# Cross attention with split fp32: three score banks and one bank of values, values scaled by one multiplication a pair, and the value burst last in TensorE's step

## The reference

```python
N, C, S, H = 16, 64, 256, 8          # after reshape; queries from x, keys and values from ctx
xn  = (x - mean(x[n])) * rsqrt(var(x[n]) + 1e-5) * gamma + beta
q   = Wq @ xn + bq                   # 8 heads of 64 channels
k,v = Wkv @ ctx + bkv
att = softmax((q * C**-0.25) . (k * C**-0.25))     # per sequence n and head, 256 x 256
y   = att . v
out = x + Wo @ y + bo
```

## Time and profile before

| | |
|---|---|
| median of 3 runs | 228.07 us (227.21 to 231.05) |
| profiled execution, first to last instruction | 228.2 us |
| busy: TensorE, VectorE, ScalarE, GpSimd | 91%, 87%, 79%, 70% |
| mean granted TensorE clock | 0.965 of full speed |

### The profile page before, as it was taken

One profiled execution on the slowest core, in us unless ns is written; L12 is line 12 of the kernel. 1 busy time (PEld: TensorE's weight loads), 2 busy tenths in 40 slices (PEclk: granted clock), 3 DMA queues, 4 the chain that ended last, 5 costly groups with the idle time before them and its releaser, 6 DMA issues.

```text
span 228.2 us, 7194 instructions
## 1 busy us (share of the span) xinstructions
PE 208.6 (91%) x2511; PEld 179.9 (79%) x2511; DVE 199.3 (87%) x589; ACT 181.1 (79%) x371; POOL 160.3 (70%) x157
## 2 busy tenths in 40 slices
PE   6968878799999999999999998999999999999872
PEld 6857757588888798889888887888888888887761
DVE  3589987879898999899999999999999998989765
ACT  2374586787889988898889888989897979888880
POOL 5135185777987877789788887789686869776460
PEclk9975897999999999999999999999999999999998
DMA  5964137480767566566665665656657656442000
GB/s 134 261 272 93 27 82 174 107 184 14 164 141 160 131 153 142 132 141 151 140 153 122 160 151 121 151 127 154 142 127 166 149 133 143 93 94 62 13 3 23
DMA packets 31090, 29.04 MB, mean 127 GB/s; under 512 B 4240, under 2 KB 29840, under 8 KB 31056
## 3 DMA queue, kind: packets, MB, share of 16 engines
q1 hardware_dynamic: 30224, 28.07, 52.4%
q10 hardware_dynamic: 832, 0.53, 1.0%
HBM read 3.80 MB, written 1.05 MB: 21 GB/s over the span
## 4 chain that ended last, share of the span: by engine, by line
PE 41%; POOL 20%; issue 13%; ACT 11%; DVE 11%; ACTq 2%; POOLq 0%; DVEq 0%
POOL p_lo L773 19%; PE ps_sc L522 6%; PE ps_max L546 6%; PE ps_sc L523 5%; PE ps_z L479 4%; ACT p_full L678 4%; DVE neg_max L894 4%; ACT p_hi L675 3%; PE ps_z L481 3%; PE ps_z L480 3%; PE ps_z L414 3%; PE ps_m L589 2%; PE ps_t L497 2%; PE ps_m L590 2%; DVE z_sum L910 2%
## 5 line engine op out<-in xcount | busy, mean ns | idle before, releaser
L773 POOL TENSOR_TENSOR p_lo<-p_full,p_hi 128x512 f16<-128x512 f32 x122 | 139.9, 1163 | 42.3 <-ACT p_full L678 41.2
L675 ACT ACTIVATE p_hi<-ps_sc 128x512 f16<-128x512 f32 x128 | 77.9, 608 | 18.3 <-PE ps_sc L523 15.9
L894 DVE TENSOR_REDUCE neg_max<-ps_max 128x2 f32<-128x512 f32 x128 | 85.9, 677 | 6.9 <-PE ps_max L546 6.8
L678 ACT ACTIVATE p_full<-ps_sc 128x512 f32<-128x512 f32 x128 | 78.7, 615 | 0.0
L522 PE MATMUL ps_sc<-t_a,c_seq 128*128 128x256 f32 x256 | 71.2, 300 | 3.5 <-issue 2.6
L523 PE MATMUL ps_sc<-t_b,c_seq 65*128 65x256 f32 x256 | 67.3, 284 | 0.0
L479 PEld LDWEIGHTS ps_z<-u_hi,p_hi 128*128 128x128 f16 x512 | 46.4, 97 | 12.8 <-issue 8.2
L479 PE MATMUL ps_z<-u_hi,p_hi 128*128 128x65 f16 x512 | 53.0, 195 | 2.2 <-DVE p_lo L930 1.9
L522 PEld LDWEIGHTS ps_sc<-t_a,c_seq 128*128 128x128 f32 x256 | 49.2, 192 | 5.9 <-issue 4.6
L480 PE MATMUL ps_z<-u_lo,p_hi 128*128 128x64 f16 x512 | 52.8, 193 | 0.0
L481 PE MATMUL ps_z<-u_hi,p_lo 128*128 128x65 f16 x512 | 52.7, 194 | 0.0
(11 more groups left out here) (108 smaller groups left out, 233.9 us busy)
## 6 DMA issues: line engine op xcount, KB each, us to landing
t_a<-t_a SPq DMA_DIRECT2D x90, 128.0 KB, 2.4
t_b<-t_b SPq DMA_DIRECT2D x30, 128.0 KB, 2.5
x_seq<-x_hi SPq DMA_DIRECT2D x15, 128.0 KB, 2.4
c_pad<-c_hi SPq DMA_DIRECT2D x30, 64.0 KB, 2.1
c_seq<-c_hi SPq DMA_DIRECT2D x15, 128.0 KB, 2.4
x_res<-x_tiles SPq DMA_DIRECT2D x4, 256.0 KB, 6.7
out<-x_res SPq DMA_DIRECT2D x16, 64.0 KB, 2.0
x_seq<-x_lo SPq DMA_DIRECT2D x15, 64.0 KB, 2.1
```

The source lines that it names most:

```text
L675: nc.scalar.activation(p_hi[:, buf, :, :].rearrange("p t s -> p (t s)"), scores, ACT.Exp).then_inc(act_phi, 1)
L678: nc.scalar.activation(p_full[:, head % 2, :], scores, ACT.Exp).then_inc(act_p, 1)
L773: nc.gpsimd.tensor_tensor(p_lo[:, buf, :, :].rearrange("p t s -> p (t s)"), p_full[:, head % 2, :], p_hi[:, buf, :, :].rearrange("p t s -> ...
L894: nc.vector.tensor_reduce(to, ps_max[:, unit % 2, :].rearrange("p (t s) -> p t s", t=KT), X, ALU.max, negate=True).then_inc(dve_max, 1)
```

## The change

The four sums of a pair get one bank; the scores get three. VectorE no longer adds each head's 64 columns to `z_sum` four times a pair. It multiplies all 256 columns of a pair by the broadcast reciprocals into a new tile `z_parts`, and one `tensor_reduce` after the second pair and one after the fourth add four, and then five, such parts. TensorE issues the value burst behind the scores and the product of its step, and VectorE scales behind the maximum of its step. The first value burst is still in step 7 (`AV_FIRST` is as before).

```diff
+SC_BUFS = 3
+        z_parts = sb("z_parts", [P, H // 2 + 1, KT, C], fp32)
-        ps_sc = ps("ps_sc", [P, 2, KT * S])
-        ps_z = ps("ps_z", [P, 2, 512])
+        ps_sc = ps("ps_sc", [P, SC_BUFS, KT * S])
+        ps_z = ps("ps_z", [P, 512])
...
-            return (ps_t[:], ps_z[:, 0], ps_z[:, 1], ps_sc[:, 0], ps_t[:], ps_z[:, 0])[turn] if turn < T_EARLY else ps_t[:]
+            return (ps_t[:], ps_z[:], ps_sc[:, 2], ps_sc[:, 0], ps_t[:], ps_z[:])[turn] if turn < T_EARLY else ps_t[:]
...
+        def sum_at(n, h):
+
+            e = av_at(*divmod(n * H + h - 1, H))
+            return (e[0], e[1] // 4) if e and e[1] % 4 == 2 else None
...
             def step(n, h):
-
-                if e := av_at(n, h):
...
-                    need(pe, dve_zsum, (m * PAIRS + first // 2 - 1) * 2 * KT)
...
-                    need(pe, act_p, m * H + head - 1)
+                    need(pe, act_p, i + 1 - SC_BUFS)
...
                     last.then_inc(pe_s1, 1)
 
+                if e := av_at(n, h):
...
+                    need(pe, dve_zpart, m * PAIRS + first // 2)
+                    lo_done(pe, m, first)
+                    lo_done(pe, m, first + 1)
...
+            def scale_values(m, first):
+                pair = first // 2
+                sums = ps_z[:, 0:4 * Z_W].rearrange("p (k t z) -> p k t z", t=KT, k=2)
+                inv = inv_sum[:, pair % 2, :].rearrange("p (k t z) -> p k t z", t=KT, k=2)
+                dve.wait_ge(pe_av, m * H + first + 2)
+                nc.vector.reciprocal(inv, sums[:, :, :, C:C + 1]).then_inc(dve_inv, 1)
+                dve.wait_ge(dve_inv, m * PAIRS + pair + 1)
+                if pair % 2 == 0:
+                    need(dve, dve_zsum, m * 2 + pair // 2)
+                nc.vector.tensor_tensor(z_parts[:, first % 4:first % 4 + 2], sums[:, :, :, 0:C], inv.broadcast_to([P, 2, KT, C]),
+                                        ALU.mult).then_inc(dve_zpart, 1)
+
+            def add_values(m, part):
+                dve.wait_ge(dve_zpart, m * PAIRS + 2 * (part + 1))
+                if part == 0:
+                    total, count = z_parts[:, H // 2], H // 2
+                    need(dve, dve_zsum, 2 * m)
+                else:
+                    total, count = z_sum[:, m % 2], H // 2 + 1
+                    dve.wait_ge(dve_zsum, 2 * m + 1)
+                    need(dve, pe_y, m - 1)
+                nc.vector.tensor_reduce(total, z_parts[:, 0:count].rearrange("p h t c -> p t c h"), X, ALU.add).then_inc(dve_zsum, 1)
...
-                if z_step:
...
-                                nc.vector.scalar_tensor_tensor(out=total, in0=part, scalar=scale, in1=total, op0=ALU.mult,
-                                                               op1=ALU.add).then_inc(dve_zsum, 1)
+                if e := sum_at(n, h):
+                    add_values(*e)
+                if e := av_at(n, h):
+                    scale_values(*e)
```

More of the change, by code:

```diff
@@ L32 @@
 T_EARLY = 6
-T_AHEAD, T_LO_AHEAD, MAX_AHEAD, AV_BEHIND = 12, 11, 11, 4
-UP_AHEAD, TB_AHEAD, DUP_AHEAD = 11, 10, 7
+SC_BUFS = 3
+T_AHEAD = 12
+T_LO_AHEAD = 11
+MAX_AHEAD = 11
+AV_BEHIND = 4
+UP_AHEAD = 11
+TB_AHEAD = 10
+DUP_AHEAD = 7
 P_BUFS = 8
@@ L413, in keep_warm @@
                 for _ in range(count):
[L414 removed]
+                    mm(ps_z[:, 0:P], ident[:], mean_w[:], start=True, stop=True)
             def products_a(bank):
@@ L502, in step @@
                     m, head = e
-                    q, b, bank = m % 2, m % C_BUFS, head % 2
+                    i = m * H + head
+                    q, b, bank = m % 2, m % C_BUFS, i % SC_BUFS
                     if head == 0:
@@ L548, in step @@
                     last.then_inc(pe_s1, 1)
+                if e := av_at(n, h):
+                    m, first = e
+                    if first == 0:
+                        pe.wait_ge(dve_ulo, 2 * (m + 1))
+                    if m == 0 and first < 4:
+                        pe.wait_ge(dve_tlo, T_EARLY)
+                    need(pe, dve_zpart, m * PAIRS + first // 2)
+                    lo_done(pe, m, first)
+                    lo_done(pe, m, first + 1)
+                    for head in (first, first + 1):
+                        buf = head % P_BUFS
+                        for qt in range(KT):
+                            qs = slice(qt * P, (qt + 1) * P)
+                            z0 = (head % 2 * KT + qt) * Z_W
+                            for kt in range(KT):
+                                u_h, u_l = u_hi[:, m % 2, kt, head, 0:Z_W], u_lo[:, m % 2, kt, head, :]
+                                mm(ps_z[:, z0:z0 + Z_W], p_hi[:, buf, kt, qs], u_h, start=(kt == 0), stop=False)
+                                mm(ps_z[:, z0:z0 + C], p_hi[:, buf, kt, qs], u_l, start=False, stop=False)
+                                last = mm(ps_z[:, z0:z0 + Z_W], p_lo[:, buf, kt, qs], u_h, start=False, stop=(kt == KT - 1))
+                        last.then_inc(pe_av, 1)
                 if h == 1 and n >= 2:
                     m = n - 2
-                    pe.wait_ge(dve_zsum, (m + 1) * H * KT)
+                    pe.wait_ge(dve_zsum, 2 * (m + 1))
                     if n < N:
@@ L671, in step @@
                     buf = head % P_BUFS
-                    scores = ps_sc[:, head % 2, :]
+                    scores = ps_sc[:, (m * H + head) % SC_BUFS, :]
                     act.wait_ge(pe_s2, m * H + head + 1)
```

23 lines of the change are left out of this document (2 added, 21 removed).

## The result

| | before | changed |
|---|---|---|
| median of the runs | 228.25 us (227.21 to 231.05) | 233.61 us (230.97 to 235.35, 4 runs) |
| changed to before | 1 | 1.020 (1.010 to 1.029) |
| profiled execution | 228.2 us span | 232.93 us, span 231.1 |
| mean granted TensorE clock | 0.965 | 0.956 |

I had forecast 225.3 us in a range of 220 to 232. The change makes the kernel slower, and the time lies outside the range.

The account below looks back on a forecast made before the run. TensorE's work plus the wait for the maxima was taken to bound the period. Terms of -2.0 (twelve periods), +0.7 (start) and -1.5 (end) sum to -2.8 from 228.07, giving 225.3 us, range 220 to 232.

Parts of the forecast that it names:

- What bounds the kernel: Steady periods of 11.93 us: TensorE issues nearly without a gap, the maxima's chain mostly hidden beside it, VectorE needing 10.7.
- the chain of the maxima: Before each sequence's first scores: ScalarE's copy and a DMA must land; 1.61 us plus landing, 4.07 on average.
- the second stretch: TensorE from a sequence's first scores to the last score matmul of h = 5: 7.01 us before, 7.65 forecast.
- The burst moves: Steady part: one burst leaves the stretch before the first scores; period 11.76 for 11.93, 2.0 us saved in 12.
- the first stretch: TensorE from the last score matmul of h = 5 to the next first scores: 4.67 us before, 4.07 forecast.
- The sign I had named: Named as showing the forecast right: TensorE idle 0.2 to 1 us ahead of nearly every h = 0 score matmul.
- VectorE's instructions: VectorE's value work per sequence: multiplications, reciprocals and two sums at 3.45 us against 3.40 before, so nothing saved.
- rival C: Slower: strided sums make VectorE the bound, deciding from about 0.9 us more a sequence; period 12.4, time 234; chance 0.12.
- One value bank at nothing: Bursts waiting for the previous pair's multiplication: covered by two steps, some 2 us, so no cost; otherwise up to 0.5 a pair.
- The start: First scores of sequence 1: a burst that ran under their wait for maxima now comes after it, +0.7 us.
- The end: Last heads: ScalarE runs through, -1.9 us; the last pair costs 0.3 to 0.4 more; net -1.5.
- The third bank at nothing: Third score bank: no gain in the steady part beyond the moved burst; its place is the end.

Follow-up runs that it names:

- e3: The kernel before with the order alone changed: burst behind the product of its step, reciprocal and additions behind the maximum; 0.996 (0.989 to 1.003) of before.
- e1: The changed kernel with both sums reading neighbouring numbers, which computes something else; 1.013 (1.004 to 1.022) of before.
- e7: The changed kernel with the first value bursts spread over the steps by the table AV_FIRST; 1.008 (1.003 to 1.013) of before.
- e9: e7 with e1's sums of neighbouring numbers on top, which computes something else; 0.991 (0.987 to 0.994) of before.
- e5: e3 with three score banks and one value bank, the four additions kept; 1.001 (0.996 to 1.007) of before.
- e4: The kernel before with only the multiplication and two sums taken over, old order and banks kept; 1.008 (1.002 to 1.014) of before.
- e2: The changed kernel with the parts innermost in z_parts: sums read neighbours, the multiplication writes 20 bytes apart; 1.011 (0.994 to 1.029) of before.
- e12: The changed kernel with the second sum of each sequence made twice, once into an unread tile; 1.132 (1.121 to 1.143) of before.
- e15: The kernel before with the copy of the maxima and its DMA moved between two exponentials of ScalarE; 1.014 (1.007 to 1.021) of before.

## Why the prediction was wrong

**What bounds the kernel.** Right in e3, where the chain of the maxima and the second stretch set the period once the burst is moved. Wrong for the changed kernel, where VectorE joins them.

**The burst moves: -2.0.** The mechanism was right. In e3 the copy stood 1.29 behind the last score matmul, as worked out; the first stretch averaged 4.07 us for the 4.07 forecast, and the second 7.75 for 7.65. The period came out at 11.82 for 11.76, a gain of 1.3 us in twelve periods. In the changed kernel the first stretch averaged 4.42 and the second 7.48, and only 0.4 is left, since the transposition waits for VectorE (4.7 us). The sign I had named, TensorE idle ahead of nearly every first score matmul, did not come: the profile marks three such waits in the twelve periods, 1.6 us. In the slow windows the scores start 3.78 and 3.84 us behind the copy at landings of 3.4 and 3.5, which is 0.35 plus the landing.

**VectorE's instructions: the step that failed.** Reciprocal and multiplication were sized right (0.20 and 0.34 for 0.21 and 0.33). The sums were not: 0.58 and 0.71 in the prediction, 1.00 and 1.22 start to start. VectorE thus took 4.4 us a sequence for the values and not 3.45, some 11.7 in a period of 11.9. I had put the sums on the line of a reduction that reads neighbours; the row against a strided price read 32 numbers from PSUM and said nothing of SBUF. Nor could so short a row decide: at e1's 0.77 ns a number, 32 numbers would cost 0.025 us more, and the row is 0.02 longer than the reciprocal beside it. The two sums cost 0.93 us a sequence more than I had counted, and TensorE paid with the 4.7 us of waits at the transposition and with the end. This is the mechanism of rival C, to which I gave 0.12: the Trainium skill had named it in the section cited there, and I let the row on PSUM outweigh the page. Its price of the step was half again too high (1.29 more a sequence forecast, 0.88 by e1). Its period of 12.4 was too high, since VectorE's extra work filled its former waits (132.6 to 140.3 us busy in twelve periods), and its point of decision, 0.9 us, was where the case fell. Between e7 and e9 the sums cost about 4 us of the time.

**One value bank at nothing: failed at the start and at the end.** The cover of two steps holds in the steady part, where the changed kernel waited once, 0.2 us. At the start, with bursts in three successive steps, TensorE waited 0.65 us for `z_parts`, and spreading them (e7) moved sequence 2 forward by 3.3 us. I had listed the wait as a sign of error and never looked at where the table places bursts closer than two steps. I had also left out the sum in that stretch. At the end the bursts waited for the bank 2.3 us in four times, and 3.1 us in e5, where VectorE still does the old additions.

**The start: +0.7.** The sign of the term was right by luck and its size wrong, +2.0 up to sequence 2. The reason given was wrong: with the order alone (e3) the start gains 0.9 and TensorE's wait ahead of the first scores of sequence 1 shrinks from 1.66 to 0.9. The loss comes with the bank, the crowd around it and the new arithmetic: of the distance between the first scores of sequences 1 and 2, e3 has 13.55, the banks alone (e5) add 0.6, and the changed kernel has 1.3 more than that.

**The end: -1.5.** The order alone gave -0.9, and the last exponential at 218.63. In the changed kernel it was +1.25: the last pair took 1.9 us where I had allowed 1.4, and two sums ahead of `p_lo` held the bursts back. I had asked what the third bank frees and not what stands ahead of `p_lo` on VectorE. Bank and sums both take part: e4, with two value banks, is 1.2 longer there than the kernel before, and e9, with cheap sums and one bank, is 27.0 against e3's 26.05. How they divide stays open.

**The third bank at nothing.** Nothing showed a gain from it: e5 is not better than e3. But e5 takes the value bank away in the same step, so the third score bank was never tried alone.

**The sum.** The span was 5.7 us above the forecast of 225.4. Spreading the bursts took 2.7 off it (e7) and cheap sums another 3.7 (e9), which ends at 224.7. So these two are as large as the whole miss. That the rest then adds up so well is partly luck, since e3 shows the terms of the start, the periods and the end each off by 0.6 to 1.6 us.

## What to carry to other kernels

Price a reduction by its inner step before its length: a row that reads neighbours, or that reads PSUM, does not carry over to SBUF at a step of 512 bytes, and a layout that turns the step around may move the same cost to the writer. When a buffer is given up, look for the place where a hand-written table lets its users follow most closely, which is here in the first steps, and at the end of the kernel, rather than at the mean distance. While an engine still has waits, added work fills them first: the period hardly shows it, and the loss appears where the engine stands on the path, at the start and the end.

## What the runs showed of the hardware that I had not expected

- A `tensor_reduce` over fp32 in SBUF with an inner step of 512 bytes took 1070 ns for 512 numbers and 1298 for 640; with neighbours 676 and 810. A `tensor_tensor` of 256 numbers took 424 ns writing pairs of rows of neighbours and 652 writing at a step of 20 bytes, while a `tensor_reduce` to 128 results took 678 ns writing at 20 bytes and 676 writing neighbours.
- At the first scores of sequence 1, after a wait of 2.6 us TensorE's granted clock read 0.50 to 0.52 for six microseconds (e1), after one of 2.3 us 0.50 (e2), after one of 1.68 us 0.56 (e12). After one of 2.0 us in e15 and of 1.66 us in the kernel before it stayed at 1.00. So the length of a wait alone doesn't tell whether the clock falls; what does is open.
- A copy with a DMA behind it, put between two instructions of ScalarE, delayed the second by 0.84 us, little more than the copy (0.25) and the issue (0.52) together.
